# A Mamba mixer: one Pool product in place of four scaled ScalarE copies, and the order of work moved on four engines

## The reference, cut to what matters

```python
zxbcdt = x @ in_proj_w.T
z, xBC, dt = split(zxbcdt)                    # z 256, xBC 512, dt 4 (one for each head)
dt = softplus(dt + dt_bias)
xBC = silu(causal_conv4(xBC) + conv_b);  xs, Bm, Cm = split(xBC)
dA = exp(-dt * exp(A_log))
h  = h * dA_t + dt_t * x_t (outer) B_t        # one state 64 x 128 for each of 4 heads
y  = h . C_t + D * x_t
y  = y * silu(z);  y = rmsnorm(y) * norm_w;  out = y @ out_proj_w.T
```

## Time and profile before

| | us |
|---|---|
| median of 3 runs (lowest to highest) | 641.08 (640.45 to 641.96) |
| the profiled execution | 639.96, its span 638.0 |
| mixer's steps 0 to 27 in it | 40.6 to 274.9 |
| PE, DVE, ACT, POOL busy | 546.5, 444.5, 360.4, 267.7 |
| mean granted TensorE clock | 0.929 |

### The profile page before, as it was taken

The page is one execution under the profiler, slowest core; times in us unless marked ns, Lnnn a source line. Parts: engine busy times, 40 slices in busy tenths (PEclk is TensorE's granted clock), DMA queues, the critical chain, the costliest instruction groups (busy, mean ns, idle before and its releaser), DMA issues.

```text
span 638.0 us, 13876 instructions
## 1 busy us (share of the span) xinstructions
PE 546.5 (86%) x3457; PEld 452.1 (71%) x3457; DVE 444.5 (70%) x1657; ACT 360.4 (56%) x1013; POOL 267.7 (42%) x324
## 2 busy tenths in 40 slices
PE   5588888898998989978789999973599999999593
PEld 3467677776777877766467877763599999999441
DVE  3746868577776657768568999997366666666267
ACT  4767584848485674834446656641266556666234
POOL 2213323241314123322102666677266666676333
PEclk9889999889998789989989999995699999999797
DMA  9399999990000000000064111111222222222383
GB/s 271 115 256 172 182 179 186 172 188 19 0 18 1 2 17 2 17 1 17 18 173 142 44 36 44 40 39 56 56 66 72 66 74 69 69 69 65 111 210 100
DMA packets 76395, 54.78 MB, mean 86 GB/s; under 512 B 10524, under 2 KB 69408, under 8 KB 76184
## 3 DMA queue, kind: packets, MB, share of 16 engines
q1 hardware_dynamic: 70352, 43.39, 33.9%
q0 software_dynamic: 4320, 8.99, 4.2%
q10 hardware_dynamic: 1640, 1.45, 0.7%
HBM read 40.62 MB, written 31.58 MB: 113 GB/s over the span
## 4 chain that ended last, share of the span: by engine, by line
PE 40%; issue 34%; DVE 11%; POOL 10%; DMA 4%; ACT 1%; ACTq 1%; POOLq 0%; SPq 0%; DVEq 0%
PE bank L1852 11%; PE bank L1870 10%; PE bank L1722 3%; PE bank L1738 3%; POOL arena L279 2%; PE bank L1728 2%; POOL arena L291 1%; POOL queue L1277 1%; DMA arena<-in_conv_w 1%; PE bank L1843 1%; POOL arena L267 1%; POOL x L297 1%; PE bank L1713 1%; POOL arena L294 1%; DVE nmx L1485 1%
## 5 line engine op out<-in xcount | busy, mean ns | idle before, releaser
L284 POOL TENSOR_TENSOR arena<-arena,half_neg 128x1 f32<-128x1 f32 x32 | 17.6, 550 | 196.0 <-ACT arena L442 196.0
L1317 POOL DMA_INDIRECT results<-arena x71 | 75.7, 1067 | 55.0 <-ACT arena L1416 50.4
L1852 PE MATMUL bank<-front,arena 128*128 128x128 f32 x568 | 78.5, 282 | 1.1 <-issue 0.3
L1870 PE MATMUL bank<-h_all,front 128*128 x568 | 75.5, 276 | 0.1
L1277 POOL DMA_INDIRECT queue<-arena,pos x64 | 63.1, 985 | 28.5 <-issue 13.8
L1852 PEld LDWEIGHTS bank<-front,arena 128*128 128x128 f32 x568 | 70.6, 195 | 4.3 <-issue 3.1
L1870 PEld LDWEIGHTS bank<-h_all,front 128*128 128x128 f32 x568 | 69.4, 193 | 0.3 <-issue 0.3
L1635 DVE COPY arena<-arena 128x516 f32 x71 | 35.9, 506 | 42.5 <-PE bank L1852 34.6
L684 PE MATMUL bank<-h_hi,wc_hi 128*128 128x512 f32 x96 | 46.6, 486 | 15.5 <-ACT arena L436 15.5
L1410 ACT ACTIVATE front<-bank 128x128 f32<-128x128 f32 x71 | 19.7, 278 | 53.6 <-PE bank L1843 52.7
L1648 DVE TENSOR_SCALAR front<-bank,arena 128x128 f32<-128x128 f32 x142 | 42.8, 342 | 4.7 <-PE bank L1852 4.5
(11 more groups left out here) (282 smaller groups left out, 1498.1 us busy)
## 6 DMA issues: line engine op xcount, KB each, us to landing
queue<-in_pad_rows SPq DMA_DIRECT2D x8, 2178.0 KB, 33.1
arena<-queue SPq DMA_DIRECT2D x71, 66.0 KB, 1.9
rows<-mod_rows SPq DMA_DIRECT2D x8, 384.0 KB, 6.3
x_keep<-x SPq DMA_DIRECT2D x8, 256.0 KB, 2.3
arena<-in_w SPq DMA_DIRECT2D x1, 2048.0 KB, 8.8
h_all<-in_w SPq DMA_DIRECT2D x1, 2048.0 KB, 8.6
h_all<-results SPq DMA_DIRECT2D x8, 256.0 KB, 4.8
arena<-results SPq DMA_DIRECT2D x8, 256.0 KB, 5.1
```

Of the source, the lines that this page charges most:

```text
L1317: pool.indirect_dma_start(k.results, bass.IndirectOffsetOnAxis(ap=xg[:, c, D:D + 1].bitcast(I32), axis=0), yw[:, c, :], None).then_inc(S[f ...
L1852: mm = t_.matmul(bank[(2 if g < NG // 2 else 6) + p][:, g * P:g * P + P], wc[:, p, g * P:g * P + P], xt[:, p, :], start=True, stop=True)
L1870: mm = t_.matmul(bank[4 + p][:, 0:D], ht[:, p, g * P:g * P + P], w2[:, e, g, :], start=(g == 0), stop=(g == NG - 1))
```

## The change

It does not change what is computed. `xdw` becomes one product on POOL. The rest is order: z0 and z1 go ahead of bank 6's turnings on PE, z2 and z3 ahead of y; ACT takes out all four z at the head of c0, and does Exp and Ln there too, after bank 6 and before flat; Exp and Silu go to the head of c1. On DVE, xdt, lt and mt stand first in each step, the totals (before L607) behind them, the dt work moves from c1 to c0, `nm1` goes behind y1, and the statistics of sequences 3 to 7 are made in halves in c0 and c1 and no longer in c2. On POOL their power goes ahead of that of the mixer's norm. The last quarter of z has three buffers in place of two (256 more columns of the arena).

```diff
 POOL, after the power of the second norm (L279), before that of the mixer's norm (L284)
+                if chunk(s) and c < 3:
+                    wait(pool, "s_xdt", s + 1)
+                    wait(pool, "s_lt", s + 1)
+                    if s >= 2:
+                        wait(pool, "s_smm", n_y(s - 1))
+                    last = lt[:, s % 2, :].rearrange("p (h i) -> p h i", h=NH)[:, :, P - 1:P]
+                    g_.tensor_tensor(hv(xdw[:, s % 2, :]), hv(xdt[:, s % 2, :]), last.broadcast_to([P, NH, HD]), ALU.mult).then_inc(S["s_xdw"], 1)
+                g = b + 3
+                if 3 <= g < NB and c == 2:
...
+                    g_.tensor_tensor(rs1[:], ve1[:], half_neg[:], ALU.pow).then_inc(S["l1_rs"], 1)
 ACT
                 if front and c == 0:
-                    z_leaves(f, 0)
-                    z_leaves(f, 1)
-                if front and c == 1:
-                    (Exp and Ln of dt)
+                    for i in range(NC):
+                        z_leaves(f, i)
                 if 0 <= g < NB and c == 2:
                     (h out)
+                if front and c == 1:
+                    wait(act, "d_dax", f + 1)
...
+                    (Exp of the decay, Silu)
                 if between:
                     between()
                 if s in turned:
                     (bank 6 out)
                 if front and c == 0:
-                    z_leaves(f, 2)
-                    z_leaves(f, 3)
-                if chunk(s) and c < 3:
-                    wait(act, "s_xdt", s + 1)
-                    wait(act, "s_lt", s + 1)
-                    for h in range(NH):
-                        ac.activation(xdw[:, s % 2, h * HD:h * HD + HD], xdt[:, s % 2, h * HD:h * HD + HD], ACT.Copy,
-                                      scale=lt[:, s % 2, h * P + P - 1:h * P + P]).then_inc(S["s_xdw"], 1)
-                if front and c == 1:
-                    (Exp of the decay, Silu)
+                    (Exp and Ln of dt)
                 if front and c == 0:
                     flat_leaves(f)
 DVE
-                if gl < NB and c == 3:
-                    (nm1)
-                if front and c == 1:
-                    (dt work, first part)
-                (xdt; dt work, second part; lt; tap; y1; mt)
+                (xdt; lt; mt)
+                if chunk(s) and c == 0:
+                    (the totals out of bank 7)
+                if front and c == 0:
+                    (dt work, first and second part)
+                (tap; y1)
+                if gl < NB and c == 3:
+                    (nm1)
...
-                if gl < NB and c == 2:
+                norm = ({2: (0, 1, 2, 3)} if gl < 3 else {0: (0, 1), 1: (2, 3)}).get(c, ()) if gl < NB else ()
+                if norm:
                     (bn_stats of those chunks)
-                if chunk(s) and c == 0:
-                    (the totals out of bank 7)
...
-                if front and c == 1:
+                if front and c == 0:
                     wait(dve, "d_ln", f + 1)
                     (dt, and then dax)
 PE
+                if front and c == 0:
+                    z(f, 0)
+                    z(f, 1)
                 if s in turned:
                     (turnings into bank 6; then the totals)
                 if front and c == 0:
-                    z(f, 0)
-                    z(f, 1)
+                    z(f, 2)
+                    z(f, 3)
...
                     (y of s-1)
-                    if front and c == 0:
-                        z(f, 2)
-                        z(f, 3)
                     if tc < 3:
-                        wait(pe, "s_xdw", NH * (n_y(t) + 1))
+                        wait(pe, "s_xdw", n_y(t) + 1)
```

More of the change, by code:

```diff
@@ L210, in hv, with z_rows @@
             return ap.rearrange("p (h o) -> p h o", h=NH)
+        def z_rows(f, i):
+            return zs[:, f % 2, i, :] if i + 1 < NC else zs_last[:, f % 3, :]
         def over_rows(ap, n):
@@ L299, in body @@
                 g = b + 3
-                if g < NB and c == 2:
+                if g < min(3, NB) and c == 2:
                     wait(pool, "l1_ve", g + 1)
@@ L329, in z_leaves @@
                     wait(act, "w_lo", 2)
-                if f >= 2:
-                    wait(act, "s_yz", NC * (f - 2) + i + 1)
+                ago = 2 if i + 1 < NC else 3
+                if f >= ago:
+                    wait(act, "s_yz", NC * (f - ago) + i + 1)
                 ac.activation(dtr[:, i * NH:i * NH + NH], bank[n % 2][:, DI:DI + NH], ACT.Copy)
-                ac.activation(zs[:, f % 2, i, :], bank[n % 2][:, 0:DI], ACT.Silu).then_inc(S["f_ev"], 1)
+                ac.activation(z_rows(f, i), bank[n % 2][:, 0:DI], ACT.Silu).then_inc(S["f_ev"], 1)
             def flat_leaves(f):
@@ L383, in body @@
                                   bias=mod[:, 0, 0, g:g + 1]).then_inc(S["f_ev"], 1)
+                if front and c == 1:
+                    wait(act, "d_dax", f + 1)
+                    act.wait_ge(S["set_pool"], 1)
+                    if f >= 1:
+                        wait(act, "o_w", seventh["da", f - 1] + 1)
+                    ac.activation(da48[:].rearrange("p (i w) -> p i w", i=3)[:, 0::2, :], dax[:].rearrange("p (o w) -> p o w", o=1).broadcast_to([P, 2, NC * NH]),
+                                  ACT.Exp).then_inc(S["d_da"], 1)
+                    ac.activation(early[:], ones[:, 0:1], ACT.Silu)
                 if between:
@@ L407, in body @@
                 if front and c == 0:
[L408 to L423 removed]
+                    if f == 0:
+                        act.wait_ge(S["w_in2"], 16 * 6)
+                        ac.activation(a_exp[:], a_log[:], ACT.Exp)
+                    wait(act, "d_neg", f + 1)
+                    ac.activation(dte[:], dtn[:], ACT.Exp).then_inc(S["d_exp"], 1)
+                    wait(act, "d_exp", f + 1)
+                    ac.activation(dtl[:], dte[:], ACT.Ln, bias=1.0).then_inc(S["d_ln"], 1)
                 if front and c == 0:
@@ L626, in body @@
                         dve.nop(nofuse=True).then_inc(S["o_r"], 1)
-                if gl < NB and c == 2:
-                    wait(dve, "l1_st", NC * (gl + 1))
-                    for i in range(NC):
+                if norm:
+                    wait(dve, "l1_st", NC * gl + norm[-1] + 1)
+                    for i in norm:
                         v.bn_aggr(mv1[:, i, :], st1[:, i, :]).then_inc(S["l1_ag"], 1)
@@ L635, in body @@
                     v.bn_stats(st2[:], x[:, t, :]).then_inc(S["l2_st"], 1)
-                if gl < NB and c == 2:
+                if norm and norm[-1] == NC - 1:
                     wait(dve, "l1_ag", NC * (gl + 1))
@@ L1076, in after_mixer @@
             late[0] += n
-            assert late[0] <= 19568
+            assert late[0] <= 19824
             return k.carve(late[0] - n, shape)
```

72 lines of the change are left out of this document (32 added, 40 removed).

## The result

The kernel with the change takes **611.90 us** (median of 4 runs, 607.35 to 613.21) against 640.84 (640.45 to 641.96, 4 runs) for the kernel before on the same chip: a ratio of 0.953 (0.949 to 0.957). It is faster, by 28.9 us where 22.6 were forecast; the time lies 6.6 us under the forecast and inside the range. The profiled execution is the lowest of the four, 607.35 us with a span of 605.5 at a mean granted clock of 0.951.

The account below looks back on a forecast made before the run. PE was taken as the bound, by its waits and half clock: 10.6 + 4.0 + 3.1 - 2.8 + 0.9 = 15.8 us plus 6.8 of clock, so 639.96 - 22.6 = 617.4, as median 618.5 us (chance 0.5), range 609 to 630.

Parts of the forecast that it names:

- 3.1: c0's balance: waits for yz, totals and z's release mostly go, a new z2 wait comes; 3.1 us gained, bounds 0.5 to 5.
- Conv 2's waits: In c2, PE's six waits for ACT's release of conv 1 go whole: 10.6 us gained.
- The cover: Conv 1 is out at 15.4, conv 2 wants it at about 17.6: 2 us to spare.
- c3 and `yz`: The five waits of c3's output for DVE's decay rows go, yz ends earlier: 4.0 us gained, bound below 3.0.
- z2's wait: In c0, a new wait of PE for z0's release behind xn1: 0.8 us (0.6 to 1.0), five times.
- c1's output: In c1, PE's output waits 0.75 us for bank 6 instead of 0.21, five times: 2.8 us lost, bounds 0 and 6.
- The product: 24 products on POOL, 0.61 us each: nothing on PE's path, bound 0.4 a product if it holds up DVE.
- the rival that it holds up DVE: POOL's product holds up DVE on the path, c3 into c0 and tails: at most 14.6 us back, 633 us, chance 0.04.
- The lead: Before the first sequence's conv 2, Exp and Ln start while flat waits for taps: 0.9 us gained, bounds 0 and 2.
- The clock: The four 3.41 us half-clock stretches behind conv 2's waits go, 4 x 1.7 = 6.8 us; the two in c0 stay.
- recovers everywhere: Rival: the clock recovers also in c0 and step 28, 6.8 and 3.4 us more: 608 us, chance 0.15.
- the slower rivals: Clock falls in c0, 628.7 us (0.2); DVE held up, 633 (0.04); conv 2's waits stay, 640 (0.04); clock stays down, 647 (0.07).

Follow-up runs that it names:

- e4: The changed kernel with one more Exp and Silu, each with its table load (2.97 us of ACT), behind bank 6's release in c1: 622.97 us, ratio 0.971.
- e6: The changed kernel with the first norm's statistics of sequences 3 to 7 back in c2 and nm1 at the head of c3: 616.61 us, ratio 0.961.
- e9: The changed kernel with mt behind y1 again on DVE, lt still ahead: 614.11 us, ratio 0.955.
- e5: The changed kernel with ACT releasing bank 6 ahead of Exp and Silu in c1: 598.69 us, ratio 0.933; again on another chip 606.65 us, 0.947.
- e11: As e5, but with the four scaled copies on ACT behind bank 6 and no product on POOL: 619.43 us, ratio 0.967.
- e7: The changed kernel with z at its old places on PE and ACT: 615.15 us, ratio 0.956.
- e1: The changed kernel with the four scaled copies back on ACT and POOL's product gone, the moves of order kept: 623.22 us, ratio 0.972.
- e2: The kernel before with POOL's product in place of ACT's four copies, nothing else moved: 628.17 us, ratio 0.979.
- e3: The changed kernel with the dt work back in c1 on ACT and DVE, the rest as changed: 627.25 us, ratio 0.976.

## Why the prediction was right, and where its sizes were off

**The mechanism** is what the prediction said it is, step by step. Its terms for the steps at full clock were 10.6 + 4.0 + 3.1 - 2.8 = 14.9 us, of which 1.2 lie in step 28, so 13.7 for steps 0 to 27; measured 14.7. That two of them missed in opposite directions is behind this agreement, and that is luck: c0 was to get 0.3 us shorter and got 1.04 shorter, c1 was to get 0.55 longer and got 1.13 longer.

- *Conv 2's waits, 10.6 us:* gone whole, as predicted. Conv 1 is out 15.2 us behind the start of c0 (169.34 less 154.17; 15.4 predicted). The cover was put at 2 us; e4 measured 2.2.
- *c3 and `yz`, 4.0 us:* the five waits for the decay rows are gone, c3 is 0.65 us shorter (0.74 predicted), and `yz` ends at c0 + 0.8 (154.97 less 154.17; 1.0 to 1.35 predicted). e6 brought both back by moving the norm alone (1.19 us and c0 + 1.35).
- *z2's wait:* predicted 0.8 with 0.6 to 1.0, measured **0.44** or 0.45 in four of the five c0 and 0.59 in the fifth. z2 asked when I said it would, at c0 + 2.83 (157.44 less 0.44, less 154.17); z0's release came earlier, with `yz`, at c0 + 3.2 (157.38), not 3.4 to 3.8. e9 shows the chain: with `mt` back in it the wait is 1.0.
- *c1's output:* predicted 0.75, measured **1.35** in six sequences. This is the term that was mis-sized for the worse: 8.0 us of waiting where I counted five of 0.75, against 1.2 in six before. There are six such steps, not five. Bank 6's release came when predicted, at c0 + 14.6 (14.8). What I had wrong was PE: I took c0 to last 7.9 us, as 7.13 of work and 0.8 of waiting, and it lasts 7.15. The earlier trace rows show 7.13 us busy in the old c0, and the new one is busy for 6.71. Part of it is that a wait also lengthens PE's busy time, as e5's lines show: c1 is busy for 6.86 us with its wait and for 6.64 without (e5), c2 for 7.77 with one (e11) and 7.51 without, and in the old order of z with next to no wait c0 takes 7.02 in all (e7). With PE there sooner, the wait for a release that comes at its own time is longer: PE asked at c0 + 13.35 (168.87 less 1.35), not at 14.1.
- *The product:* 0.62 us each on POOL (0.61 predicted), and nothing waits for it. Of the rival that it holds up DVE a little is seen: the tap of c1 that starts beside it took 0.83 us in six sequences, taps with nothing beside them 0.73 to 0.75. That is 0.1 us once in a sequence, under the bound of 0.4, and off PE's path. Once it went the other way: the product that began 0.13 us behind a tap (53.12 behind 52.99) took 1.09 us, and the tap its usual 0.74.
- *The lead:* 2.3 us where 0.9 stood. Its low stretches changed place as well, and in the experiments that have the same lead step 0 stands at 39.6 to 40.1, so some 1.5 of it is one execution's luck.
- *The clock,* the term that failed in size: 4 x 1.7 = 6.8 us were predicted, 13.6 measured in steps 0 to 27 of the profiled execution. The other three lost 5 to 7 us more to the clock than this one (see the result), so at the median the miss is smaller. I left the two stretches of c0 because a wait stands there still. It does, 0.44 + 0.21 us, and the clock stays up. The rival "recovers everywhere" (608 us) described the mixer better than the forecast did. Its other part, 3.4 us for the stretch of step 28, did not come: that stretch is gone, but there are three of 3.41 us at 258.9, 276.0 and 289.6, in step 30 and behind the mixer, where before there was one of 3.41 besides it, so 10.2 us of low clock stand there as before. Why the clock stays up in c0 is open.

For the profiled pair the forecast was 10.0 us short (22.6 against 32.6): 6.8 of them are the clock in the mixer, 1.4 the lead, 1.0 the steps at full clock and 0.7 what comes behind the start of step 28.

So the forecast's 0.5 and this rival's 0.15 share the result: 611.9 us lies between 618.5 and 608. None of the slower rivals came up in the change itself; a clock that falls at the end of c1 and in c2 came up in e1 instead, whose c1 holds a wait of 2.30 us.

**What each part is worth,** for the most part by taking it back (mixer at full clock, and its low stretches in the one profiled execution, us):

| kernel | full clock | low | ratio |
|---|---|---|---|
| before | 220.6 | 27.3 | 1 |
| the change | 205.9 | 0 | 0.953 |
| without the product (e1) | 212.4 | 20.5 | 0.972 |
| only the product (e2) | 216.9 | 6.8 | 0.979 |
| dt work in c1 (e3) | 213.7 | 17.1 | 0.976 |
| norm in c2 (e6) | 210.3 | 17.1 | 0.961 |
| `mt` behind y1 (e9) | 209.1 | 0 | 0.955 |
| z at its old places (e7) | 206.3 | 3.4 | 0.956 |
| bank 6 first (e5, twice) | 196.3 | 0 | 0.933, 0.947 |
| bank 6 first, no product (e11) | 207.2 | 0 | 0.967 |

## What to carry to other kernels

List what stands in an engine's queue in front of each release, not only how busy the engine is: ACT is busy for 56% of the span, yet two orders of the same work of it differ by 9.6 us (the change and e5). When a wait has two chains of nearly one length behind it, ACT's copies and DVE's dt work here, taking one away shows only the small difference between them (e2), and its price shows when the other is gone. Count a wait at somewhat more than its idle time: the matmul in front of it no longer overlaps its successor, and the clock may be lower in a kernel with longer waits (e1).

## What the runs showed of the hardware

- **The length of a wait does not settle the clock.** In steps 0 to 27: before, with 1.78 us waits in c2, the clock was low in six places; e1, with 2.30 in c1, in four; e3, with 1.35 and then 1.6, in three; e6, with 1.2 and 1.0, in four. e2 kept a wait of 1.48 in five c2 and had one low stretch, in a c0; the change kept 1.35 in c1 and e11 1.25 in c2, and both had none, e7 1.52 with one of 3.4 us at step 0. So waits of 1.2 to 1.8 us stand here beside both clocks, and these runs don't settle what decides between them. Each is one execution; those of one kernel differ too (0.940 to 0.951 for the change).
- **A tiny DVE instruction lasted as long as its neighbour on POOL.** L649 (a `tensor_scalar`) adds a constant to 128x4 numbers; its shortest was 0.17 us, and at 170.38 it took 1.25, to 171.63, beside POOL's L308, which ended at 171.61. This is what the earlier trace rows showed of L521, in a new place; it delays nothing that PE needs (PE is busy for 7.50 of c2's 7.50 us). SBUF — State Buffer in the Trainium skill (Who interferes with whom) names single-input instructions of this form too among those that can take the pair of ports shared with GpSimd; the row agrees.
- **A wait costs PE more than the idle time that is shown:** 1.35 us of waiting lengthened c1 by 1.57 (the change against e5), 1.25 us lengthened c2 by 1.51 (e11 against e5), 0.79 us by 1.07 (e4 against the change), so 0.2 to 0.3 us each. In c1 0.16 us of the 0.22 lie in front of the wait, as the overlap of the last matmul with its successor (0.39 us long, the next one 0.23 behind its start in e5), and some 0.07 behind it.
